# First stage of a gated cross-attention block: weight halves before the row list, four tiles of keys before their values

## The reference

```
x = x + tanh(g_xattn[0]) * L0_xattn(layernorm(x), ids, ctx)          # by id: silu-like (h * sigmoid), two products
x = x + tanh(g_ffn[0])   * L0_ffn(layernorm(x), shared, routed ...)  # top 4 of 16
x = x + tanh(g_xattn[1]) * L1_xattn(layernorm(x), ctx, Wq, Wk, Wv)   # k = rmsnorm(ctx @ Wk.T), v = ctx @ Wv.T
x = x + tanh(g_ffn[1])   * L1_ffn(layernorm(x), splines ...)
```

## Time and profile before

| | us |
|---|---|
| median of 3 runs | 1210.96 |
| lowest and highest run | 1209.52, 1215.19 |
| profiled execution, device time | 1215.63 |
| its span, first to last instruction | 1213.7 |
| PE, DVE, ACT, POOL busy in the span | 1000.1, 701.0, 668.1, 525.0 |

### The profile page before, as it was taken

How to read it: one execution, slowest core, us unless ns; L and a number is a source line. 1 busy time by engine, 2 the same in 40 slices (tenths; PEclk the granted TensorE clock), 3 DMA queues, 4 the chain that set the end, 5 groups by cost and what they waited for, 6 DMA issues and landing times. The chain is left out here.

```text
span 1213.7 us, 27956 instructions
## 1 busy us (share of the span) xinstructions
PE 1000.1 (82%) x9519; PEld 573.2 (47%) x9520; DVE 701.0 (58%) x1710; ACT 668.1 (55%) x1085; POOL 525.0 (43%) x453
## 2 busy tenths in 40 slices
PE   3699989969899878899999999915899877988841
PEld 1455556446577656577777777702122211211121
DVE  7676755578887457322223222215477788776776
ACT  4555645454454257444445444416688867899920
POOL 0232232156676264455556555422223444343452
PEclk9899999989899989999999999967799988999965
DMA  7343231389984496666676666672877767576212
GB/s 253 113 164 117 87 124 63 137 206 193 228 197 127 160 340 148 140 117 116 119 150 117 116 120 117 102 153 82 154 152 149 176 137 166 119 169 137 54 41 70
DMA packets 183460, 170.81 MB, mean 141 GB/s; under 512 B 137140, under 2 KB 138740, under 8 KB 182452
## 3 DMA queue, kind: packets, MB, share of 16 engines
q1 hardware_dynamic: 150082, 110.03, 35.4%
q0 software_dynamic: 25856, 56.39, 24.2%
q10 hardware_dynamic: 7426, 3.12, 1.1%
HBM read 80.78 MB, written 65.19 MB: 120 GB/s over the span
## 5 line engine op out<-in xcount | busy, mean ns | idle before, releaser
L1982 ACT ACTIVATE sb_atp<-ps_atpS 128x1024 f32<-128x1024 f32 x256 | 243.2, 1036 | 48.8 <-PE ps_atpS L1710 48.8
L1410 PEld LDWEIGHTS ps_shpH<-sb_roxT,sb_rowt 128*128 (+1 forms) x2844 | 169.0, 107 | 20.5 <-DVE sb_roxT L1277 1.9
L1410 PE MATMUL ps_shpH<-sb_roxT,sb_rowt 128*128 128x128 f16 (+1 forms) x2844 | 173.5, 220 | 1.7 <-DVE sb_roxT L1277 1.7
L1399 PE MATMUL ps_shpY<-sb_rowt,sb_rohhl 128*128 (+1 forms) x711 | 170.8, 386 | 4.2 <-DVE sb_rowt L1290 3.7
L1722 PE MATMUL ps_atpO<-sb_atp,sb_atv 128*17 128x512 f32 x1024 | 139.6, 618 | 30.9 <-ACT sb_atp L1982 20.8
L1034 POOL DMA_INDIRECT sb_roxg<-xn,sb_roentry x79 | 86.6, 1097 | 92.6 <-DMA sb_roentry<-list 68.1
L1133 ACT ACTIVATE sb_roh<-ps_shpH,sb_rob 128x128 f32<-128x128 f32 (+1 forms) x237 | 68.9, 362 | 104.6 <-PE ps_shpH L1410 101.0
L1399 PEld LDWEIGHTS ps_shpY<-sb_rowt,sb_rohhl 128*128 128x128 f16 (+1 forms) x711 | 67.6, 99 | 73.2 <-issue 9.8
L1122 ACT ACTIVATE sb_roy<-ps_shpY,sb_roentry 128x512 f32<-128x512 f32 x79 | 54.2, 686 | 78.3 <-PE ps_shpY L1399 72.7
L1022 POOL DMA_INDIRECT list<-sb_shentry,sb_shposb x64 | 72.9, 1139 | 35.2 <-DVE sb_shposb L1205 20.2
L1041 POOL DMA_INDIRECT x2a<-sb_roy,sb_roentry x40 | 65.1, 1627 | 42.4 <-ACT sb_roy L1122 40.0
(11 more groups left out here) (347 smaller groups left out, 1801.9 us busy)
## 6 DMA issues: line engine op xcount, KB each, us to landing
sb_rowt<-rw SPq DMA_DIRECT2D x15, 768.0 KB, 10.7
sb_rowt<-rw SPq DMA_DIRECT2D x15, 704.0 KB, 7.9
kst<-sb_kykp SPq DMA_DIRECT2D x16, 512.0 KB, 3.1
qst<-sb_quqp SPq DMA_DIRECT2D x12, 512.0 KB
vst<-sb_kyvt SPq DMA_DIRECT2D x16, 272.0 KB
sb_stage<-ctxT SPq DMA_DIRECT2D x4, 1024.0 KB, 7.1
sb_shxin<-x SPq DMA_DIRECT2D x16, 256.0 KB, 7.2
xn<-sb_shxhl SPq DMA_DIRECT2D x16, 256.0 KB, 5.6
```

The lines of the kernel that those rows point to most:

```text
L1399: last = e.matmul(pY[it.p][:, :], hhl[it.p][0:n, x, k * P:(k + 1) * P], weight(value, 2 * W1 + w + k * D, n, D), start=j == 0, stop=j == l ...
L1410: last = e.matmul(rpH[it.p][0:n, f * P:(f + 1) * P], weight(ex["up"], w + k * FF + f * P, P, n), rxT[it.p][:, x + k, :], start=j % (3 * KD ...
L1982: S.done(e.activation(pr[n % 6][:, :], pS[n % 3][:, :], ACT.Exp, scale=HD ** -0.5 / SA ** 2), "atexp")
```

## The change

- DVE makes the low halves of jobs 0 and 1 (Wk, context block 0) right behind the comparison of the ids, ahead of the count's evaluation; the low half of job 2 (Wv) goes behind the 0/1 matrices. ACT makes the high halves of jobs 0 and 1 ahead of the gates (tanh), and job 2 behind them.
- PE makes the keys of tiles 0 to 3 ahead of the list product, then the values of tiles 0 to 3. For these tiles the PSUM bank goes by the tile's parity (`bank`), for keys and values alike.
- ACT evacuates the four keys with job 3 between the third and fourth, then values 0, job 4, values 1; in beat 1 values 2, job 5, values 3. In beat 2 `rows` stands ahead of `evacuate`.
- DVE sums the squares of tiles 0 to 3 all ahead of beat 1. The low halves of jobs 4 and 5 stand at the ends of beats 2 and 3, where they stood at the ends of beats 1 and 2.

```diff
@@ Keys
+    def bank(self, n, half):
+        return (self.pK, self.pV)[n % 2 if n < KEY_FIRST else half]
@@ project
-        e.wait_ge(S.sem("sulo"), (3, 4, 5, 6)[n // 4] if n or half else 2)
-        if half:
+        e.wait_ge(S.sem("sulo"), (3, 4, 5, 6)[n // 4] if n >= KEY_FIRST or half else 2)
+        if n < KEY_FIRST:
+            if half and n >= 2:
+                S.wait(e, "kyvt", turn_of(n - 2))
+            else:
+                S.wait(e, "kyraw", turn_of(n - 2 + 4 * half))
+                S.wait(e, "kysq", turn_of(n - 2 + 4 * half))
+        elif half or n == KEY_FIRST:
             S.wait(e, "kyvt", turn_of(n - 1))
@@ scalar
+        for j in range(2):
+            self.job_high(e, j)
         e.wait_ge(S.sem("su_gates"), 16)
...
-        for j in range(3):
-            self.job_high(e, j)
+        self.job_high(e, 2)
...
-        for n in range(KEY_FIRST - 1):
+        for n in range(KEY_FIRST):
             keys.evacuate(e, n)
-            keys.values(e, n)
-            self.job_high(e, 3 + n)
+            if n == 2:
+                self.job_high(e, 3)
+        keys.values(e, 0)
+        self.job_high(e, 4)
+        keys.values(e, 1)
...
+            if b == 2:
+                rows(b - 1)
             if 0 <= b - 2 < N1:
                 evacuate(b - 2)
-            if b - 1 < N1:
+            if b - 1 < N1 and b != 2:
                 rows(b - 1)
...
             if b == 1:
-                keys.evacuate(e, KEY_FIRST - 1)
-                keys.values(e, KEY_FIRST - 1)
+                keys.values(e, 2)
+                self.job_high(e, 5)
+                keys.values(e, 3)
@@ vector
+        for j in range(2):
+            self.job_low(v, j)
         v.wait_ge(S.sem("su_count"), 1)
...
-        for j in range(3):
-            self.job_low(v, j)
...
+        self.job_low(v, 2)
         v.wait_ge(S.sem("su_listed"), 1)
...
-        keys.squares(line, v, 0)
-        self.job_low(v, 3)
-        keys.squares(line, v, 1)
+        for n in range(KEY_FIRST):
+            keys.squares(line, v, n)
+            if n == 0:
+                self.job_low(v, 3)
...
-            if b <= 2:
-                keys.squares(line, v, 1 + b)
-                self.job_low(v, 3 + b)
+            if b in (2, 3):
+                self.job_low(v, 2 + b)
@@ tensor
-        for n in range(2):
-            for half in range(2):
-                keys.project(e, n, half)
+        for n in range(KEY_FIRST):
+            keys.project(e, n, 0)
         e.wait_ge(S.sem("su_places"), 1)
...
-        for n in range(2, KEY_FIRST):
-            for half in range(2):
-                keys.project(e, n, half)
+        for n in range(KEY_FIRST):
+            keys.project(e, n, 1)
```

More of the change, by code:

```diff
@@ L341, in project @@
         at = (n // 4) * W + (n % 4) * P
-        out, w, name = ((self.pK, self.part["wk"], "kyk"), (self.pV, self.part["wv"], "kyv"))[half]
-        e.wait_ge(S.sem("sulo"), (3, 4, 5, 6)[n // 4] if n or half else 2)
-        if half:
+        out, (w, name) = self.bank(n, half), ((self.part["wk"], "kyk"), (self.part["wv"], "kyv"))[half]
+        e.wait_ge(S.sem("sulo"), (3, 4, 5, 6)[n // 4] if n >= KEY_FIRST or half else 2)
[6 more added lines that the diff above has]
+        elif half or n == KEY_FIRST:
             S.wait(e, "kyvt", turn_of(n - 1))
@@ L358, in evacuate @@
         S.wait(e, "kyn", turn_of(n - 4))
-        S.done(e.activation(self.raw[n % 4][:, :], self.pK[:, :], ACT.Copy, scale=1.0 / SW ** 2), "kyraw")
+        S.done(e.activation(self.raw[n % 4][:, :], self.bank(n, 0)[:, :], ACT.Copy, scale=1.0 / SW ** 2), "kyraw")
         if n >= KEY_FIRST:
             S.wait(e, "kyms", turn_of(n - 1))
-        S.done(e.activation(self.squared(n), self.pK[:, :], ACT.Square, scale=1.0 / SW ** 2), "kysq")
+        S.done(e.activation(self.squared(n), self.bank(n, 0)[:, :], ACT.Square, scale=1.0 / SW ** 2), "kysq")
     def values(self, e, n):
@@ L368, in values @@
         S.done(e.activation(self.vt[n % 4][:, :].rearrange("p (h d) -> p h d", d=HD + 1)[:, :, 0:HD],
-                            self.pV[:, :].rearrange("p (h d) -> p h d", d=HD), ACT.Copy, scale=self.K["gate"][:, 7:8]), "kyvt")
+                            self.bank(n, 1)[:, :].rearrange("p (h d) -> p h d", d=HD), ACT.Copy, scale=self.K["gate"][:, 7:8]), "kyvt")
     def squared(self, n):
```

## The result

The changed kernel takes 1205.95 us (median of 8 runs) beside 1212.31 for the kernel before on the same chip: a difference of 6.4. The ratio on record is 0.9952, with a 95% interval of 0.9933 to 0.9972: faster by 0.48%, or 5.8 us, where 8.0 (0.66%) were forecast. The time lies 2.9 above the forecast of 1203.0 and inside its range of 1200.0 to 1208.0. The profiled execution took 1207.71, span 1205.9, beside 1215.63. The first stage became 6.6 us shorter, not 8.0: DVE's last statistics start at 192.1 instead of 198.7.

The account below looks back on a forecast made before the run. PE bounds the first stage's loop; before it fills, PE's first down, released by DVE, counts. 4.6 (indices) + 3.0 (tile 1) + 0.9 (square sum) - 0.5 (turn) = 8.0; 1210.96 - 8.0 = 1203.0 us, range 1200.0 to 1208.0.

Parts of the forecast that it names:

- Step 1 and 2, start and row list: Before the loop: PE's first projection at 13.8, 5.5 us earlier; row indices at 28.05, 4.6 earlier; gather at 28.98.
- Step 3, the first gather: First gather on POOL, held until DVE's low half of job 3 ends: again 3.16 us, tile 0 taken up at 34.9.
- The bound that I gave the term: First gather's time: 2.1 us less if the gather comes first, 1.5 more if job 5's load slows it.
- Step 4, tiles 1 and 2: DVE starts tile 1 at 38.5, 7.6 us earlier, and tile 2 at 44.3, 8.5 earlier.
- Step 5, down(0): PE's first down, as the loop fills, at 54.4 in place of 62.92, 8.5 us earlier.
- A pause of 0.4 to 0.5: PE's wait at the turn of tile 3 for DVE's low half; counted as 0.5 us lost, not growing.
- Sum: Whole kernel: 4.6 (indices) + 3.0 (tile 1) + 0.9 (square sum) - 0.5 (turn of tile 3) = 8.0 us gained.
- Job 5's load: Rival: the load, issued at 27.57, delays tile 1; 8.0 used up at 19 us from issue; chance 0.03.
- The clock rival: PE's clock falls in the 26.5 pause or is low at down(0) and the next projection; 1206.3 us; chance 0.06.
- The prediction's 1.2 GHz for the first projection: PE's first projection took 4.53 us where a later one takes 2.75, read as the price of the low clock.
- The gain not arriving: Rival: a later stage's own limit takes the gain back; gain 0 to 4, 1209 us; chance 0.12.

Follow-up runs that it names:

- The start alone: The changed kernel with DVE's square sums of tiles 2 and 3 and low halves of jobs 4 and 5 back in beats 1 and 2; ratio 0.9971.
- experiment 1: The changed kernel with DVE's low half of job 5 moved into DVE's idle gap ahead of h(0) in the same beat; ratio 0.9926.
- first kernel of experiment 6: The changed kernel with DVE's low half of job 3 moved behind the square sums of tiles 1 to 3; ratio 0.9942.
- experiments 1, 6 and 7: experiment 1; then, on the changed kernel, job 3's low half later (0.9942), also job 5's load and small tables later (0.9919); down reusing up's expert register (0.9863).

## Why the prediction was right, and which step failed

- **Step 1 and 2, start and row list: right.** First projection 13.92 (forecast 13.8), indices 28.06 (28.05), gather 28.98 (28.98). The start alone was worth 4.4 (forecast 4.6).
- **Step 3, the first gather: right in number, and the reading shown.** Held behind the low half it took 3.17 (forecast 3.16); with the low half elsewhere 1.13, so the 3.17 was not the gather's own. The Trainium skill, "SBUF — State Buffer", section "Who interferes with whom", has DVE's operations with two on-chip inputs block only GpSimd work that reads that memory, and infers that writing descriptors doesn't. The 3.17 and 1.13 show that the gather is blocked, which the prediction took to go against the page. But the gather also reads its row indices from on-chip memory (`sb_l1idx`), which would be the page's own case; no run here separates that reading from the writing. The bound that I gave the term, 2.1 less if the gather comes first, was wrong: with 2.0 less on the record, nothing was gained until the load of job 5 and the small tables were out of the way too.
- **Step 4, tiles 1 and 2: right.** 38.61 and 44.44 (38.5, 44.3). ACT's order is worth 0.7 of it at tile 2 (45.15 without it).
- **Step 5, down(0): right (54.64, forecast 54.4); "A pause of 0.4 to 0.5": the term that failed.** The wait at the turn itself was shorter, 0.20. But with it, the sequencer loses the work it does ahead under 12 wide products when it isn't held. Between experiment 1 and the changed kernel, from start to start: projection to turn 2.60 and 2.95 (0.35 more), turn to up(2) 0.44 and 0.87 (0.43), up(2) to down(1) 3.80 and 5.21 (1.41). Together 2.19, and the stage differed by 2.3. The term stood in the sum with 0.5. The step counted how late data came and took the durations of PE's instructions as fixed; and up(0) and up(1), which have no wide products ahead of them, could have warned: they took 3.8 to 5.3 us in every kernel here with computed addresses, up(1) 4.27 in the changed kernel at a granted clock of 1.00. I had put that down to the lower clock there.
- **Sum.** 8.0 forecast, 6.6 in the first stage: the term's 2.2 in place of 0.5 makes 6.3 of it. The timing's 5.8 (0.48% of 1212) has an interval of 3.4 to 8.1, which holds both. So the direction and the range came out right with one term four times too small; of the 2.9 by which the time was missed, 1.35 is the kernel before, whose median of 8 runs was 1212.31 in place of 1210.96. The range was drawn over the gather and the clock, and that it also had room for this cost was luck.
- **Rivals.** Job 5's load landed in 4.9 us, not 19. The clock rival, at 0.06, named two places, the pause at 26.5 and down(0) with the projection behind it: the granted clock was 1.00 at both (the four projections of values took 10.53). It did fall between them: 0.66 granted from 40 to 50 us, after PE had waited 0.70 and 3.20 us with one turn of 8 small products between. It cost nothing visible: turn(2) started at 49.01, its rows ready at 48.96, and where up(0) took only 3.91 in place of 5.11 (first kernel of experiment 6) turn(2) came at 48.95. It was back at 1.00 from 50 us on. The kernel before had such a drop too (a mean of 0.57 granted from 46 to 54 us). The pause of 3.20, and the row of 40 to 50 us (clock: third number from the end):

```profile
42.65 1.01 PE L277 MATMUL ps_shpY<-sb_ident,sb_l1xhl 128*128 128x128 f16 x8 [3.20 <-ACT sb_l1xT L582]
```

```profile
40.00:50.00 10.00, 6.83 (x66) 6.28 (x66) 7.08 (x10) 7.20 (x10) 2.90 (x4) 0.66 0.59 201
```

The Trainium skill's warning in "TensorE: Matmul & The Clock Gate", section "HAM oscillation — how this bites in real kernels", was thus borne out as to the clock, not as to the price. The prediction's 1.2 GHz for the first projection (4.53 us) is a reading of the duration alone: the profile gives a granted clock of 1.00 for 19 to 24 us.
- **The gain not arriving: no.** No later stage took the gain back: by experiments 1, 6 and 7 what the first stage gains or loses, the kernel does, within the intervals.

## What to carry to other kernels

A short wait on PE can cost more than its length when what follows is bound by issue (here 2.2 us for 0.2): ask whether the instructions behind it take their addresses from registers, and look in the trace for the same instruction behind a wait. A pause "put down to nothing" that comes back in every beat is worth a look at the sequencer's own operations; here it hid a register load of 0.3 to 0.9 us a beat, and taking it away was worth more than the whole change (11.4 us of the stage beside 6.6). And a move that makes one thing earlier by taking another's slack should be put into a gap that the trace shows idle, not behind the instruction that frees the next engine.

## What the runs showed of the hardware

- Issue: 48 narrow products whose weights have computed addresses, with two address operations (46 and 32 ns) to every three weight loads, took 4.16 us behind a wait, 0.26 for three. With fixed addresses the same 48 products took 2.84, 59 ns each. With the first address operation 1.4 us ahead of the first weight load, under wide products, they took 2.90.
- A load of a register from on-chip memory took PE's sequencer 0.30 us at the median and up to 0.89, with 0.17 behind it for the two steps that follow, and the pauses of 16 downs that went with it were 0.8 on average (12.6 us in all).
- A gather's record on POOL, beside DVE's operation with two on-chip inputs, took 3.17 us and ended 1.0 behind it; 1.13 without it.
- The gather's data took 5.8 us from issue beside a 1 MB load and small tables, 3.5 without.
